# Two Mamba stages of a twelve-layer kernel: a new order of work and new accumulator banks

## The reference, cut to what matters

```python
xz = x @ in_proj_w.T                    # 512 columns: 256 for x_p, 256 for z
xc = silu(causal_conv4(x_p) + conv_b)   # 256 channels, 4 taps
dt = softplus(xc @ dt_proj_w.T + dt_proj_b)
B, C = split(xc @ x_proj_w.T, 2)        # 16 and 16
s  = sum(xc * dt, -1)
y  = sum(s * B * C, -1) + xc * D_param
x  = x + (y * silu(z)) @ out_proj_w.T
```

```python
h = deltaA_t * h + dBu_t                # a scan along the rows, for each of 16 states
y = sum over the 16 states of h * C_t
y = (y + x_c * Dp) * silu(z)
out = y @ out_proj_w.T                  # then norms, an FFN and a last projection
```

## Time and profile before

| what | value |
|---|---|
| median of 3 runs | 3781.47 us (3780.93 to 3781.89) |
| the profiled execution | 3782.95 us, its span 3781.2 us |
| TensorE, VectorE, ScalarE, GpSimd busy | 86%, 70%, 53%, 16% of the span |
| first Mamba, from the first chunk's first convolution to the last chunk's first | 1447.06 to 1665.90 us |
| second Mamba, first scan to last scan | 2062.2 to 2541.2 us |

### The profile page before, as it was taken

One profiled execution on the slowest core, in us unless ns is written; L12 is line 12 of the kernel. 1 busy time (PEld: TensorE's weight loads), 2 busy tenths in 40 slices (PEclk: granted clock), 3 DMA queues, 4 the chain that ended last, 5 costly groups with the idle time before them and its releaser, 6 DMA issues. The chain is left out here.

```text
span 3781.2 us, 44076 instructions
## 1 busy us (share of the span) xinstructions
PE 3252.6 (86%) x14333; PEld 1973.0 (52%) x14402; DVE 2656.9 (70%) x6064; ACT 2003.4 (53%) x3428; POOL 588.2 (16%) x484
## 2 busy tenths in 40 slices
PE   4999999999899997679988777777899998589998
PEld 3775343443477663236544233334467776357776
DVE  5566877776455686567766878886777777777776
ACT  2444656556444444344434646453367776147776
POOL 0000000000000000000001444340023332013332
PEclk9999999999999998779999888898999999789999
DMA  2000101010100230002332000002321010011111
GB/s 76 1 28 16 44 18 36 22 39 10 29 2 1 80 96 26 1 17 88 96 107 76 1 1 0 1 1 79 123 86 41 30 45 26 1 36 30 45 46 48
DMA packets 89645, 146.25 MB, mean 39 GB/s; under 512 B 13084, under 2 KB 25564, under 8 KB 89288
## 3 DMA queue, kind: packets, MB, share of 16 engines
q1 hardware_dynamic: 89416, 143.43, 12.1%
HBM read 134.02 MB, written 9.34 MB: 38 GB/s over the span
## 5 line engine op out<-in xcount | busy, mean ns | idle before, releaser
L358 POOL TENSOR_TENSOR norm_rstd<-norm_rstd,minus_half 128x4 f32<-128x4 f32 x144 | 174.2, 1210 | 2267.6 <-DVE norm_rstd L349 2265.0
L952 ACT ACTIVATE main_tiles<-banks 128x512 f32<-128x512 f32 (+3 forms) x768 | 356.6, 489 | 246.1 <-PE banks L940 165.9
L821 DVE TENSOR_REDUCE gate_scratch<-banks 128x1 f32<-128x512 f32 (+3 forms) x608 | 367.5, 656 | 123.4 <-PE banks L771 95.7
L2179 ACT ACTIVATE main_tiles_r<-banks,feature_cols 128x512 fp32r<-128x512 f32 x512 | 352.8, 689 | 191.4 <-PE banks L228 169.2
L2187 DVE TENSOR_TENSOR main_tiles_r<-main_tiles,main_tiles_r 128x512 fp32r<-128x512 f32 x512 | 383.5, 764 | 70.0 <-ACT main_tiles L2180 68.4
L226 PE MATMUL banks<-normed_pairs,moe_weights 128*128 128x512 f32 x800 | 408.6, 511 | 17.4 <-ACT main_tiles L2180 6.8
L2180 ACT ACTIVATE main_tiles<-banks,feature_cols 128x512 f32<-128x512 f32 x512 | 349.8, 683 | 0.0
L227 PE MATMUL banks<-normed_pairs,moe_weights 128*128 128x512 f32 x800 | 318.7, 398 | 0.0
L228 PE MATMUL banks<-normed_pairs,moe_weights 128*128 128x512 f32 x800 | 318.4, 398 | 0.0
L2224 POOL TENSOR_TENSOR normed<-normed,main_tiles 128x512 f32<-128x512 f32 x128 | 217.6, 1700 | 539.4 <-DVE main_tiles L2213 539.4
L226 PE MATMUL banks<-main_tiles_r,moe_weights 128*128 128x512 f32 x640 | 267.0, 417 | 28.3 <-DVE main_tiles_r L2187 26.5
(11 more groups left out here) (333 smaller groups left out, 6831.7 us busy)
## 6 DMA issues: line engine op xcount, KB each, us to landing
main_tiles<-gates_d SPq DMA_DIRECT2D x400, 256.0 KB, 3.3
weight_staging<-in_w SPq DMA_DIRECT2D x33, 256.0 KB, 3.7
parts_d<-bf_parts SPq DMA_DIRECT2D x48, 128.0 KB, 1.8
q_stacks<-parts_d SPq DMA_DIRECT2D x192, 32.0 KB
k_stacks<-parts_d SPq DMA_DIRECT2D x192, 32.0 KB
x_res<-in_x_t SPq DMA_DIRECT2D x8, 256.0 KB, 3.3
out_x<-x_res SPq DMA_DIRECT2D x8, 256.0 KB, 3.9
rope<-in_rope SPq DMA_DIRECT2D x1, 1024.0 KB
```

The lines of the kernel that those rows point to most:

```text
L821: eng.tensor_reduce(o, bank[:, 0:per * (k1 - k0)].rearrange("p (n c) -> p n c", n=per), AX.X, ALU.max).then_inc(s.ring_free)
L952: eng.activation(weight_tile(e)[:, 0:C - q0], psum[:, 4 + e % 2, 0:C - q0], ACT.Exp, scale=HD ** -0.5).then_inc(s.at_exp)
L2179: eng.activation(pair_3(j)[0], psum[:, 2 + j % 2, :], ACT.Relu, bias=bias)
```

## The change

In the first Mamba the chunks are planned 21 us apart instead of 25, four sets of tiles are in turn instead of three, and each stage's generator is split into four, one for each chunk modulo 4. The sums leave banks 4 and 5: bs goes to bank 2, bg to bank 3, out to bank 5. A `ring` for each bank decides which use waits for which. The planned times inside a chunk grow (x from 32.4 to 49.5). MoE 1's second pass begins 44 instead of 21.5 after the last chunk's start. In the second Mamba yd, yz, out and its copy are planned 4 to 5 us earlier, and the state sums 0.4 us later. No arithmetic instruction is added or taken away, and no DMA.

```diff
@@ MoE 1, the first items of the second pass
             if k == 64:
-                eng.wait_ge(*ma_act(7, "sz1"))
+                eng.wait_ge(*ma_dve(7, "gm"))
+            if k == 65:
+                eng.wait_ge(*ma_act(7, "g"))
...
             if k == 64:
-                eng.wait_ge(*ma_dve(7, "gm"))
+                eng.wait_ge(*ma_dve(7, "m0"))
             if k == 65:
-                eng.wait_ge(*ma_act(7, "g"))
+                eng.wait_ge(*ma_dve(7, "x"))
...
                 if k == 64:
-                    eng.wait_ge(*ma_dve(7, "x"))
+                    eng.wait_ge(*ma_dve(7, "ct"))
@@ the first Mamba
-    MA_US = 25.0
-    T_MA = m1_at[-1] + M1_CHUNK + 2.0
+    MA_US, MA_LANES = 21.0, 4
+    T_MA = m1_at[-1] + 21.0
...
-        norms.append(Norm(ma_at[i] - 14.0, ("ma", i), lambda c=c: chunk(c), x_ready[c], None, None, None, None, None))
+        norms.append(Norm(ma_at[i] - 15.0, ("ma", i), lambda c=c: chunk(c), x_ready[c], None, None, None, None, None, 1.25))
...
+    MA_BANKS = {2: (("in0", 0.0, "dve", "conv0"), ("gate0", 6.8, "act", "sz0"), ("bs", 31.0, "dve", "gm")),
+                3: (("in1", 1.0, "dve", "conv1"), ("gate1", 10.2, "act", "sz1"), ("bg", 35.0, "act", "g")),
+                4: (("dt0", 13.2, "dve", "m0"),), 5: (("dt1", 15.2, "dve", "m1"), ("out", 46.5, "dve", "x")),
+                6: (("bc", 17.5, "dve", "ct"),)}
+    MA_STEP = {name: (bank, after) for bank, uses in MA_BANKS.items() for name, after, _, _ in uses}
+    ma_bank = {}
+    for bank, uses in MA_BANKS.items():
+        ma_bank.update(ring([(ma_at[i] + after, (i, name), (ma_dve if who == "dve" else ma_act)(i, step))
+                             for i in range(NC_) for name, after, who, step in uses], (bank,)))
...
-            yield ma_at[i] + 21.6
+            yield ma_at[i] + MA_STEP["bs"][1]
+            eng.wait_ge(*ma_bank_free(i, "bs"))
             eng.wait_ge(*ma_dve(i, "dt1"))
-            eng.matmul(psum[:, 4, :], ones[:, :], ma_tile(i, "m0"), start=True, stop=False)
+            eng.matmul(psum[:, 2, :], ones[:, :], ma_tile(i, "m0"), start=True, stop=False)
...
-    plan_moe1(ma_at[-1] + 21.5)
+    plan_moe1(ma_at[-1] + 44.0)
@@ the second Mamba
-            ("dt", 44.5, "dve", "m"), ("out", 130.0, "act", "oc"), ("f0", 170.0, "dve", "k0"), ("f1", 173.0, "dve", "k1"),
+            ("dt", 44.5, "dve", "m"), ("out", 125.6, "act", "oc"), ("f0", 170.0, "dve", "k0"), ("f1", 173.0, "dve", "k1"),
...
-            yield t0 + 132.0
+            yield t0 + 128.0
...
-            yield t0 + 127.0
+            yield t0 + 122.4
...
-            yield t0 + 128.5
+            yield t0 + 123.6
...
-        for q, i, n, when in state_items(6.4):
+        for q, i, n, when in state_items(6.8):
```

More of the change, by code:

```diff
@@ L1485, in ma_tile @@
     def ma_tile(i, name):
-        return wa_t[:, 8 * (i % 3) + ("xc0", "xc1", "sz0", "sz1", "a0", "m0", "a1", "m1").index(name), :]
-    def pe_ma_front(eng):
-        for i in range(NC_):
-            for step, name, bank in ((0.0, "in0", 2), (1.1, "in1", 3), (5.5, "gate0", 2), (9.0, "gate1", 3)):
-                yield ma_at[i] + step
+        return wa_t[:, 8 * (i % MA_LANES) + ("xc0", "xc1", "sz0", "sz1", "a0", "m0", "a1", "m1").index(name), :]
+    MA_BANKS = {2: (("in0", 0.0, "dve", "conv0"), ("gate0", 6.8, "act", "sz0"), ("bs", 31.0, "dve", "gm")),
+                3: (("in1", 1.0, "dve", "conv1"), ("gate1", 10.2, "act", "sz1"), ("bg", 35.0, "act", "g")),
+                4: (("dt0", 13.2, "dve", "m0"),), 5: (("dt1", 15.2, "dve", "m1"), ("out", 46.5, "dve", "x")),
+                6: (("bc", 17.5, "dve", "ct"),)}
@@ L1492, in pe_ma_front @@
+    def pe_ma_front(eng, chunks):
+        for i in chunks:
+            for name in ("in0", "in1", "gate0", "gate1"):
+                bank, after = MA_STEP[name]
+                yield ma_at[i] + after
                 if name == "in0":
@@ L1494, in pe_ma_front, with act_ma_front @@
                         eng.wait_ge(s.nat_in, 48)
-                        eng.wait_ge(s.m1_h1, 64)
-                    else:
-                        eng.wait_ge(*ma_act(i - 1, "sz0"))
                     eng.wait_ge(*normed(("ma", i)))
-                elif name == "in1":
-                    if i:
-                        eng.wait_ge(*ma_act(i - 1, "sz1"))
-                else:
-                    eng.wait_ge(*ma_dve(i, "conv0" if name == "gate0" else "conv1"))
+                eng.wait_ge(*ma_bank_free(i, name))
                 w = N1["in"] + {"in0": 0, "in1": 1, "gate0": 2, "gate1": 3}[name] * P
                 eng.matmul(psum[:, bank, :], w1n[:, w:w + P], xn(("ma", i)), start=True, stop=True).then_inc(ma_pe(i, name)[0])
-    def act_ma_front(eng):
-        for i in range(NC_):
+    def act_ma_front(eng, chunks):
+        for i in chunks:
             for blk in range(2):
-                yield ma_at[i] + 1.6 + 1.1 * blk
+                yield ma_at[i] + 1.9 + 1.1 * blk
                 eng.wait_ge(*ma_pe(i, f"in{blk}"))
@@ L1590, in pe_ma_back, with act_ma_back @@
                 w = N1["o"] + k * P
-                z = eng.matmul(psum[:, 6, :], w1n[:, w:w + P], x, start=k == 0, stop=k == 1)
+                z = eng.matmul(psum[:, 5, :], w1n[:, w:w + P], x, start=k == 0, stop=k == 1)
             z.then_inc(ma_pe(i, "out")[0])
-    def act_ma_back(eng):
-        for i in range(NC_):
+    def act_ma_back(eng, chunks):
+        for i in chunks:
             a0, a1 = ma_tile(i, "a0"), ma_tile(i, "a1")
-            yield ma_at[i] + 12.8
+            yield ma_at[i] + 16.0
             eng.wait_ge(*ma_pe(i, "dt0"))
             eng.activation(a0, psum[:, 4, :], ACT.Abs, bias=col("m1dtb", 0)).then_inc(ma_act(i, "abs0")[0])
-            yield ma_at[i] + 14.9
+            yield ma_at[i] + 18.2
             eng.wait_ge(*ma_pe(i, "dt1"))
@@ L1614, in act_ma_back, with dve_ma_back @@
             eng.activation(a0[0:16, :], psum[0:16, 6, :], ACT.Copy).then_inc(ma_act(i, "bt")[0])
-            yield ma_at[i] + 25.0
+            yield ma_at[i] + 37.2
             eng.wait_ge(*ma_pe(i, "bg"))
-            eng.activation(a0, psum[:, 5, :], ACT.Copy).then_inc(ma_act(i, "g")[0])
-    def dve_ma_back(eng):
-        for i in range(NC_):
+            eng.activation(a0, psum[:, 3, :], ACT.Copy).then_inc(ma_act(i, "g")[0])
+    def dve_ma_back(eng, chunks):
+        for i in chunks:
             a, m = (ma_tile(i, "a0"), ma_tile(i, "a1")), (ma_tile(i, "m0"), ma_tile(i, "m1"))
@@ L1850, in build @@
         x_ready[c] = lambda i=i: mb_dve(i, "x")
-    def mb_lanes(part):
-        return [lambda eng, lane=lane: part(eng, range(lane, NC_, LANES)) for lane in range(LANES)]
     def pe_mb(eng, chunks):
```

102 lines of the change are left out of this document (52 added, 50 removed).

## The result

The changed kernel takes **3713.81 us** (median of 3, 3713.15 to 3716.03) against 3781.47: 67.7 us less, ratio 0.9823 with a 95% interval of 0.98 to 0.9845. The forecast was 3700, range 3674 to 3742. The profiled execution is the 3713.15 one (before: 3782.95), so the traces differ by 69.8 us.

A forecast was written before the change was run, and what follows sets the result against it. Both Mambas were taken to run at the pace of a loop of waits, no engine full. Savings of 57, 2, 3 and 20 us sum to 82, from 3781.5 to 3699.5, called 3700 us; range 3674 to 3742.

The forecast's parts named there:

- The loop of the first Mamba: First Mamba's seven pitches: out's wait goes, bs waits for dt1; 162 against 218.8 us, 57 less (bounds 13 to 80).
- The start: Start of the first Mamba: in0 stands before MoE 1's last second matmuls instead of behind them; 2 us less.
- The table loads: ScalarE in the first Mamba: still three table loads a chunk, 1.28 us apiece, without the skill's 2.66 us per switch.
- The hand-over: First Mamba's end into MoE 1: same state about 41 us after the last conv0, against 44 before; 3 us less.
- its own sign: First Mamba's end: the forecast is wrong if MoE 1's stream starts more than 46 us after the last conv0.
- The second Mamba: Chunk boundaries: early yd ends TensorE's wait, 3.8 us less at each of five; 20 us in all (bounds 5 and 31).
- B: Rival, first Mamba: TensorE's clock stays low between waits, pitch 29, total 3753 us; chance 0.12.
- A: Main case, whole kernel: the terms as summed, 3700 us, own range 3684 to 3718; chance 0.58.
- C: Rival, first Mamba: VectorE-bound, TensorE stays at the high clock, pitch 20, total 3673 us; chance 0.12.
- D: Rival, second Mamba: gives nothing back, g and zb stay late and other chains take the gain; 3720 us; chance 0.12.
- E: Rival, first Mamba: slower, new banks tie in0 to the previous chunk's gm, pitch 36, total 3790 us; chance 0.04.
- F: Rival, whole kernel: no effect, the order does not change where it matters; chance 0.02.

The follow-up runs named there:

- bs_behind_gate1: The changed kernel with bs of the first Mamba planned at 31.6 instead of 31.0, so it follows gate1 on TensorE; 3711.45 us.
- after: The changed kernel of this study itself, with no further edit; 3713.81 us.
- bs_g_and_addf: The changed kernel with bs behind gate1, and in the second Mamba g behind the fourth state's zb and its addition behind the fourth scan; 3698.72 us.
- seven like kernels: after, norm_later, bs_behind_gate1, last_out_bank6, start_later, bank6_start_early and gate1_four_times, all with the same second Mamba instructions; its scans take 465.4 to 472.3 us.
- start_later: The changed kernel with MoE 1's second pass planned 48.5 instead of 44 us after the last Mamba chunk; 3719.75 us.
- norm_later: The changed kernel with norm and gates of MoE 1's second chunk behind the first Mamba planned 5 us later; 3716.51 us.
- bank6_start_early: The changed kernel with the last Mamba chunk's out in bank 6 and MoE 1's second pass planned 40 instead of 44 us after that chunk; 3718.82 us.
- gate1_four_times: The changed kernel with bs behind gate1, plus three more computations of gate1 into its own bank; 3723.40 us.
- last_out_bank6: The changed kernel with out of the last first-Mamba chunk in bank 6, as in the kernel before; 3714.43 us.

## Why the prediction was right where it was, and wrong where it was not

**The loop of the first Mamba: right.** Forecast for the seven pitches 162, measured 159.5; the last conv0 forecast near 1607, measured 1603.55. The path was right in its parts: the wait before bs 4.6 (forecast 4.9), bs 3.5 us from its start to gate1's (1516.43 to 1519.97; forecast 3.4), gate1 wholly at the low clock where I had taken half (1.9 against 1.4), out's wait 0.7 (forecast under 1.5). Behind gate1 the steps add up as well: norm-back ends 17.8 us after conv0 (forecast 16.8), m0 starts at 19.1, and from there VectorE's string to the next conv0 takes 4.7. The forecast had left m0 out of that string and put 0.6 for hand-overs in its place. The first pitch, 16.4, was 2 shorter than I took it. bs_behind_gate1 confirms the step on which it rested: take gate1 from behind bs, and the pitch falls by 1.6 on average. The start gave 1.3 us instead of 2; the 3.0 of the traces hold 1.7 of spread.

**The table loads: right by the trace.** The timeline of ScalarE after:

```profile
1600.07 1.28 ACT L1616 ACT_TABLE_LOAD   x1
1601.37 1.15 ACT L1616 ACTIVATE mamba_tiles<-mamba_tiles 128x512 f32<-128x512 f32 x2
```

From load to result 1.30 us, and three loads a chunk as forecast. The 2.66 us a switch that the Trainium skill gives (ScalarE: Activation LUTs, What ACT_TABLE_LOAD costs) would have made the period some 4 us longer by the forecast's working; it did not come.

**The hand-over: wrong, and the largest error.** The term "3 us less" was 9.1 more, 12 us of the 13.8 by which the forecast is too low. The step that failed is the path of the last chunk: dt1 at 28.4 (measured 31.0), gm at 33 (38.4), x at 39 (49.4). From dt1 to x I had given 10.6 us, costing the chain as if the queues were its own; it took 18.4, and in the kernel before it had taken 17.9 (1689.95 to 1707.84), so the figure could have been read. In the trace there stand in it bs at the low clock again, norm-in, a norm-back for which TensorE waits 3.04, eight small gate records and out at the low clock in 3.37 us. Besides, I had taken all of the last pitch before, 35.1 us, for the loop, though 4.4 of it came with work of MoE 1 that had to go somewhere. I had written that the forecast would be wrong if MoE 1's stream started over 46 us behind the last conv0; by the same mark as the 44 of before, the triple behind the first third matmul (1657.56), it starts at 54.0. By its own sign, then, the forecast was wrong here.

**The second Mamba: right in kind, too large in size.** No sum waits for yd, and yd meets a ready sum; but the scans gave 13.0 us against 20 forecast, with 4.4 more in the rest, part of which is the spread that the table shows (226.6 to 230.2). Per boundary it is 2.2 us (19.0 to 16.8), not 3.8. The third gap fell as forecast, from 8.2 to 9.7 us to 5.1 to 6.7 (forecast near 5.5); what failed stands around it. Two things in "yz ends 2236.9, out 2237.8, the first sum 2238.6" failed. I moved yd and yz ahead of the second scan at no cost, and they cost it 1.8 us (first gap 2.9 to 4.7). And I took out and the sum at the high clock, though TensorE waits 2.7 us before out: 2.04 and 1.92 us instead of 1.0 each. G, forecast at 3.4, takes 3.6 to 4.0.

**The rivals.** *B*, the clock stays low, fell: 0.86, not 0.78, and a pitch of 23.8. Its rule, from the Trainium skill (TensorE: Matmul & The Clock Gate, HAM oscillation), that bursts parted by waits pay the low clock each time, does hold for bs in every full period (2.04 and 1.91 us behind waits of 4.0 to 5.0); it set the size of the pitch but not its sign. Before out of the second Mamba it holds at some boundaries and not at others (last section). B was also priced too high: its saving of 13 us goes with seven full pitches of 29 to 30, though by A's rule the first two lack the back halves. With 18.5 and 23 for these, B comes to about 3737, inside the range. *C*, VectorE-bound, fell: VectorE is busy 17.1 of 23.8 us and stands 5.81 before m0, and most of what is added on TensorE shows in the pitch. *D* was nearer for the second Mamba than I gave it: about half of the forecast gain per boundary did not come. *E* and *F* fell.

The sum: 57, 2, 3 and 20 forecast. In the traces 59.3, 3.0, -9.1 and 13.0, with 4.4 in the rest and -0.8 elsewhere, 69.8; between the medians 67.7. That the total lies only 14 us off owes something to luck: the start and the scans of this execution are near the good end of what their instructions show in the other kernels.

## What to carry to other kernels

Overlapping chunks more deeply buys pitch and sells latency: cost the last chunk of the overlapped stage separately, with every instruction of its neighbours' queues in it, before booking a gain at the stage's end, and hold each piece of a forecast chain against the length that it has in the rows of before. See what foreign work stands in the last period before you call all of it the loop. When a consumer is moved earlier to free a producer, count what it passes on its own engine, and write down who is late next (here yz, then GpSimd's product, then the addition of g); an order edit pays only if both ends of the hand-over move. Judge such an edit by its own stage in the trace, as an untouched later stage can shift by several microseconds.

## What the runs showed of the hardware that I had not expected

The same wait does not always cost the clock. Before out of the second Mamba TensorE stands 2.69 us in after and in bs_g_and_addf alike, with the same four records of 0.38 to 1.02 us ahead of the wait; behind it out and the sum take 2.04 and 1.92 us in the one and 1.10 and 1.02 in the other (rows above). In after itself waits of 2.13 us are followed by 2.01 us at 2245.56 and by 1.10 at 2308.78. The third gap of its boundaries is 5.8, 6.7, 5.6, 5.1 and 5.6 us with one instruction order.

That fits the spread of a stage that nobody edited. TensorE executes the same 971 records in the scans of all seven like kernels. Where they take 465.4 us (start_later), it is busy 352.9 us at a granted clock of 0.88; where they take 472.3 (bs_behind_gate1), 362.8 us at 0.86. The lengths come in sets, too: norm_later, bank6_start_early and gate1_four_times have the same gaps to 0.1 us and take 468.6 to 468.7, after and last_out_bank6 466.0 and 466.1. What decides which set a kernel falls into, no run shows. By this spread the 9.7 us won in the first Mamba of bs_behind_gate1 showed as 2.4 in the median, and its four runs lie 10.4 us apart.
